# Cross-attention layer on one core: keys of two batches in one product, end columns projected ahead, block values written by DMA

## The reference, cut to what matters

```python
# 1 cross attention: 16 heads of 16 over 257 context rows, masked
k = memory @ wk.T ; v = memory @ wv.T ; q = rmsnorm(ln(x)) @ wq.T
x = x + sigmoid(h @ wg.T) * (softmax(q k^T * scale + mask) v @ wo.T)
# 2 causal self attention over 32 rows: 16 query heads, 4 key heads, rms norm and rotary on q and k,
#   ternary weights
x = x + rms_norm(attn(ln(x) @ w_qkv.T)) @ w_proj.T
# 3 feed forward of 704 with 8-bit activations and ternary weights
x = x + bitlinear(silu(bitlinear(ln(x), w1)) * bitlinear(ln(x), w3), w2)
```

## Time and profile before

| what | value |
|---|---|
| median of three runs | 576.29 us (575.0 to 815.79) |
| the profiled execution | 573.81 us |
| its span, first to last instruction | 572.0 us |
| mean granted TensorE clock | 0.993 |
| instructions | 20510 |
| DMA | 42.34 MB, mean 74 GB/s |

### The profile page before, as it was taken

One profiled execution on the slowest core, in us unless ns is written; L12 is line 12 of the kernel. 1 busy time (PEld: TensorE's weight loads), 2 busy tenths in 40 slices (PEclk: granted clock), 3 DMA queues, 4 the chain that ended last, 5 costly groups with the idle time before them and its releaser, 6 DMA issues. The chain is left out here.

```text
span 572.0 us, 20510 instructions
## 1 busy us (share of the span) xinstructions
PE 537.9 (94%) x7142; PEld 449.1 (79%) x7142; DVE 445.7 (78%) x1389; ACT 425.1 (74%) x1208; POOL 323.4 (57%) x490
## 2 busy tenths in 40 slices
PE   7898999999999999999999999999999999987785
PEld 6687788788887888888888878888888877865564
DVE  2667585888978787888979787878879776889664
ACT  5987898697878878787977787787878777773221
POOL 5241848566565748566555658475665648372610
PEclk9999999999999999999999999999999999999988
DMA  8532503214233231413142332414142404000000
GB/s 253 182 94 100 144 21 101 58 49 102 59 84 81 71 83 37 126 32 90 54 107 59 77 78 46 117 33 107 39 103 58 105 5 113 21 13 21 24 9 10
DMA packets 42805, 42.34 MB, mean 74 GB/s; under 512 B 16080, under 2 KB 33488, under 8 KB 42704
## 3 DMA queue, kind: packets, MB, share of 16 engines
q1 hardware_dynamic: 42704, 41.03, 27.3%
HBM read 38.26 MB, written 2.75 MB: 72 GB/s over the span
## 5 line engine op out<-in xcount | busy, mean ns | idle before, releaser
L874 ACT ACTIVATE pr<-sm,nb 128x257 f32<-128x257 f32 x256 | 129.2, 508 | 9.4 <-DVE nb L1110 8.0
L662 POOL TENSOR_TENSOR cTl<-cx,cTh 128x516 fp32r<-128x516 f32 x64 | 84.3, 1317 | 75.1 <-ACT cTh L771 75.0
L1110 DVE CUSTOM_DVE_ANT_0 sm<-x_ps,mbias 128x257 f32<-128x257 f32 x256 | 99.3, 419 | 21.9 <-PE x_ps L1416 20.2
L771 ACT ACTIVATE pt<-x_ps 128x512 f32<-128x512 f32 x112 | 65.3, 599 | 10.5 <-PE x_ps L1426 6.9
L1426 PE MATMUL x_ps<-tab,pr 128*128 128x128 f32 x512 | 71.4, 274 | 0.8 <-DVE o L1141 0.4
L771 ACT ACTIVATE kk<-x_ps 128x257 f32<-128x257 f32 x128 | 49.5, 389 | 22.1 <-PE x_ps L1308 22.1
L1426 PEld LDWEIGHTS x_ps<-tab,pr 128*128 128x128 f32 x512 | 57.3, 141 | 5.8 <-issue 4.4
L1308 PE MATMUL x_ps<-cTh,wkTh 128*128 128x258 f32 x256 | 59.7, 315 | 0.4 <-ACT pt L771 0.3
L670 POOL TENSOR_TENSOR sr<-sv,halfneg 128x20 f32<-128x20 f32 x16 | 56.7, 3541 | 1.3
L1308 PE MATMUL x_ps<-wvTh,cTh 128*128 128x256 f32 x256 | 56.8, 303 | 0.0
L1308 PE MATMUL x_ps<-cTl,wkTh 128*128 128x258 f32 x256 | 51.4, 282 | 0.6 <-POOL cTl L662 0.6
(11 more groups left out here) (193 smaller groups left out, 1342.7 us busy)
## 6 DMA issues: line engine op xcount, KB each, us to landing
cx<-in_ctx SPq DMA_DIRECT2D x64, 258.0 KB, 3.9
mbias<-mask_bias SPq DMA_DIRECT2D x64, 128.5 KB, 3.4
xq<-in_x SPq DMA_DIRECT2D x16, 128.0 KB, 2.9
xr<-in_x SPq DMA_DIRECT2D x16, 128.0 KB, 2.8
vx<-end_values SPq DMA_DIRECT2D x64, 32.0 KB, 2.3
vr<-self_values SPq DMA_DIRECT2D x64, 32.0 KB, 1.9
out<-yo SPq DMA_DIRECT2D x16, 128.0 KB, 2.6
fraw<-in_L_ffn_w SPq DMA_DIRECT2D x2, 704.0 KB, 5.2
```

What stands on the lines that cost most here:

```text
L662: g.tensor_tensor(cxbuf(cT[1], b)[:, :, :], cx[:, b % BT, :, :], cxbuf(cT[0], b)[:, :, :].bitcast(F32), ALU.subtract).then_inc(A_ctl, 1)
L771: return sc.activation(dst, src, ACT.Copy)
L874: sc.activation(pr[:, b % 2, gr, :], sm[:, b % 2, gr, :], ACT.Exp, bias=nb[:, n:n + 1], scale=-1.0, accum_out=st[:, 0, b, gr:gr + 1]).then ...
L1110: v.tensor_tensor_reduce(out=sm[:, b % 2, gr, :], in0=xb(f"S{b}", gr)[:, 0:LK], in1=mbias[:, b, :], scale=1.0, scalar=0.1 * NEG, op0=ALU.a ...
```

## The change

1. The context arrives with 256 columns a batch in place of 258 (the 257th and a zero). cTh and cTl have four buffers in place of two, and kk too; two neighbouring batches lie side by side, and one product of 512 columns makes the keys of both. K 1 m are batches 2 and 3 of the tile, K 2 m batches 0 and 1 of the next; K 0 m is batch 1 of tile 0 alone. So the repeated part has 24 K products of 512 columns for 48 of 258, and 4 copies of 512 columns on ScalarE for 8 of 257.
2. The keys of the 257th row are projected once for all 64 batches at the start (P_kx, 12 products of 64 columns, copied to kxs). GpSimd copies two batches' end columns from kxs into kk ahead of the query block of the first of the two. The load of the end columns and their rounding come before those of wv.
3. vr and vbd go. The four DMAs of B_shuffle write straight into blocks in wraw (free after the start), in turn into two of them, which one memset (VZ, in tile 0) has cleared. D_PV waits for the DMAs.
4. All lists, the banks and the dummy products are new: 261 dummy products for 167.

```diff
-        cx = sb("cx", [P, BT, 2, LKP])
-        cT = [sb("cTh", [P, 2, 2, LKP], F32R), sb("cTl", [P, 2, 2, LKP], F32R)]
+        cx = sb("cx", [P, BT, 2, LM])
+        cT = [sb("cTh", [P, 2, BT, LM], F32R), sb("cTl", [P, 2, BT, LM], F32R)]
-        kk = sb("kk", [P, 2, 2, LKP])
+        kk = sb("kk", [P, 2, BT, LKP])
+        kxs = sb("kxs", [P, 2, B])
...
+        def pair_of(tensor, k, p):
+            return tensor[:, k, 2 * p % BT:2 * p % BT + 2, 0:LM]
+        def vbd(n):
+            return wraw[:, n % 2 * 2:n % 2 * 2 + 2, :, :].rearrange("p a k (b c) -> p (a k) b c", b=BT)
...
-                        if due(i - 1):
-                            sp.wait_ge(B_vbd, i - 1)
+                        if due(i - 2):
+                            sp.wait_ge(B_pv, i - 2)
+                        else:
+                            sp.wait_ge(W_vz, 1)
                         for h in range(4):
-                            sp.dma_start(vr[h * S:(h + 1) * S, :, :],
+                            sp.dma_start(vbd(i)[h * S:(h + 1) * S, h, :, :],
...
+                if b % 2 == 0:
+                    if due(16 * i + 4 * b - 8):
+                        pool.wait_ge(A_ttr, 16 * i + 4 * b - 8)
+                    elif b == 0:
+                        pool.wait_ge(W_kx, 1)
+                    g.tensor_copy(kk[:, :, b:b + 2, LM:LK].rearrange("p m b c -> p m (b c)"),
+                                  kxs[:, :, BT * i + b:BT * i + b + 2]).then_inc(A_ke, 1)
+                    pool.wait_ge(A_ke, 2 * i + b // 2 + 1)
...
-            def k_out(i, b, m, ps):
+            def k_out(i, p, m, ps):
+                act.wait_ge(A_kp, 4 * i + 2 * p + m + 3)
+                if due(16 * i + 8 * p - 8):
+                    act.wait_ge(A_ttr, 16 * i + 8 * p - 8)
+                copy(pair_of(kk, m, p), ps[:, :].rearrange("p (b c) -> p b c", b=2)).then_inc(A_kh, 1)
...
+            def kproj(i, p, m, ps):
+                if m == 0:
+                    pe.wait_ge(A_ctl, 4 * i + 2 * p + 2)
+                split3(ps[:, :], lambda z, k2: wkT[z][:, k2, m * P:(m + 1) * P],
+                       lambda z, k2: pair_of(cT[z], k2, p)).then_inc(A_kp, 1)
...
-                        pe.wait_ge(A_kh, 8 * i + 2 * b + 2)
+                        pe.wait_ge(A_kh, 4 * i + (2 + 2 * b if i == 0 and b < 2 else 4 if b < 2 else 6))
...
-                        pe.wait_ge(B_vbd, i1)
+                        pe.wait_ge(L_vr, 64 * i1)
...
-                                          vbd[:, b * KV + j, :, :].rearrange("p h d -> p (h d)"), start=True, stop=True)
+                                          vbd(i1)[:, :, b, j * HD:(j + 1) * HD], start=True, stop=True)
```

```diff
+ pe first: (0, "K", 0, 0), (0, "S", 0), (0, "K", 0, 1), (0, "V", 1), (0, "GATE"), (0, "K", 1, 0), (0, "S", 1),
...
+ pe each:
+            ("S", 0), ("B_st",), ("C_xT",), ("D_QT",), ("D_kT",), ("V", 1), ("D_S",), ("S", 1), ("B_O",),
+            ("C_z", 0), ("K", 1, 0), ("B_oT",), ("K", 1, 1), ("PT", 0, 0), ("B_wo",), ("PT", 0, 1), ("V", 2),
+            ("S", 2), ("PV", 0), ("PT", 1, 0), ("PT", 1, 1), ("GATE",), ("B_xT",), ("C_z", 1), ("S", 3), ("B_qkv",),
+            ("C_z", 2), ("PV", 1), ("D_PV",), ("Q_h",), ("V", 3), ("PT", 2, 0), ("D_yT",), ("K", 2, 0),
+            ("PT", 2, 1), ("Q_q",), ("C_hT",), ("D_pj",), ("PV", 2), ("C_y",), ("K", 2, 1), ("PT", 3, 0),
+            ("PT", 3, 1), ("V", 4), ("PV", 3),
+ act each, end:
+            ("EXP", 3, 1), ("EXP", 3, 2), ("EXP", 3, 3), ("C_hT",), ("V", 3), ("Q_q",), ("K", 2, 0), ("B_keep",),
+            ("PT", 3, 0), ("K", 2, 1), ("PT", 3, 1), ("V", 4),
+ dve each, middle:
+            ("S", 1, 2), ("S", 1, 3), ("C_z", 0), ("D_s3",), ("Q_stats",), ("B_wo",), ("B_x1",), ("D_dn",),
+            ("C_h", 0), ("S", 2, 0), ("S", 2, 1), ("S", 2, 2), ("B_norm",), ("D_p3",), ("S", 2, 3), ("Q_norm",),
...
- pe last:  (17, "C_xT"), (17, "D_kT"), (17, "D_QT"), (17, "C_z", 0), (17, "D_S"),
+ pe last:  (17, "D_kT"), (17, "D_QT"), (17, "D_S"), (17, "C_xT"), (17, "C_z", 0), (17, "C_z", 1), (17, "C_z", 2),
- dve last: (16, "D_xstats"), (16, "D_xq", 0), (16, "D_xq", 1), (16, "D_xq", 2), (17, "D_scale"), (17, "D_kT"),
+ dve last: (16, "D_pj"), (17, "D_scale"), (16, "D_xstats"), (17, "D_kT"), (16, "D_xq", 0),
...
 SPARE: (17, "C_xT"): 32 -> 10, (17, "D_PV"): 28 -> 32, (18, "C_xT"): 32 -> 37, (18, "C_hT"): 28 -> 33
        and new ones before D_QT, D_kT, D_S, C_z
```

More of the change, by code:

```diff
@@ L34 @@
 LKP = LK + 1
+LM = LK - 1
 BT = P // S
@@ L58 @@
 BANK = {
[L59 to L62, removed]
[3 rows of a table removed]
-    "P_k1": (3,), "P_v": (4,), "P_vx": (5,),
+    "V1": (6,), "V2": (3,), "V3": (2,), "V4": (1,), "B_O": (0,), "B_oT": (3,), "B_wo": (5,), "B_xT": (5,),
+    "B_qkv": (5,), "D_QT": (1,), "D_kT": (3,), "D_S": (1,), "D_PV": (4,), "D_yT": (3,), "D_pj": (1,), "C_xT":
+    (6,), "C_z0": (6,), "C_z1": (2,), "C_z2": (6,), "C_hT": (4,), "C_y": (4,), "GATE": (6,), "Q_h": (5,), "Q_q":
[5 rows of a table added]
 }
@@ L104 @@
+            (2, "PT", 2, 0), (2, "K", 2, 0), (2, "D_pj"), (2, "PT", 2, 1), (2, "K", 2, 1), (2, "PT", 3, 0),
+            (2, "PV", 2), (2, "PT", 3, 1), (2, "V", 4), (2, "PV", 3),
         ],
         "each": [
-            ("S", 0), ("K", 1, 0), ("K", 1, 1), ("C_xT",), ("B_st",), ("D_kT",), ("V", 1), ("B_O",), ("D_QT",),
-            ("PT", 0, 0), ("PT", 0, 1), ("D_S",), ("S", 1), ("B_oT",), ("K", 2, 0), ("K", 2, 1), ("B_wo",),
-            ("S", 2), ("PV", 0), ("C_z", 0), ("V", 2), ("PT", 1, 0), ("K", 3, 0), ("B_xT",), ("PT", 1, 1),
@@ L127 @@
-            (15, "V", 3), (15, "PT", 2, 1), (15, "C_hT"), (15, "D_pj"), (15, "C_y"), (15, "PV", 2),
-            (15, "PT", 3, 0), (15, "PT", 3, 1), (16, "B_st"), (15, "PV", 3), (15, "GATE"), (16, "C_xT"),
-            (16, "B_O"), (16, "C_z", 0), (16, "C_z", 1), (16, "B_oT"), (16, "D_kT"), (16, "D_QT"), (16, "B_wo"),
-            (16, "D_S"), (16, "C_z", 2), (16, "B_xT"), (16, "B_qkv"), (16, "D_PV"), (16, "D_yT"), (16, "C_hT"),
-            (16, "D_pj"), (16, "C_y"), (17, "C_xT"), (17, "D_kT"), (17, "D_QT"), (17, "C_z", 0), (17, "D_S"),
@@ L132 @@
-            (17, "C_z", 1), (17, "C_z", 2), (17, "D_PV"), (17, "D_yT"), (17, "C_hT"), (17, "D_pj"), (17, "C_y"),
-            (18, "C_xT"), (18, "C_z", 0), (18, "C_z", 1), (18, "C_z", 2), (18, "C_hT"), (18, "C_y"),
+            (14, "S", 0), (14, "B_st"), (14, "D_QT"), (14, "D_kT"), (14, "V", 1), (14, "D_S"), (14, "S", 1),
+            (14, "B_O"), (14, "C_xT"), (14, "K", 1, 0), (14, "B_oT"), (14, "K", 1, 1), (14, "B_wo"),
+            (14, "PT", 0, 0), (14, "PT", 0, 1), (14, "S", 2), (14, "C_z", 0), (14, "V", 2), (14, "PV", 0),
@@ new lines @@
+            (14, "PT", 1, 0), (14, "C_z", 1), (14, "PT", 1, 1), (14, "B_xT"), (14, "D_PV"), (14, "GATE"),
[3 rows of a table added]
+            (15, "D_kT"), (14, "V", 4), (15, "B_st"), (14, "PV", 3), (15, "D_QT"), (15, "S", 1), (15, "D_S"),
[5 rows of a table added]
+            (16, "B_st"), (15, "PV", 3), (15, "D_pj"), (15, "GATE"), (16, "B_O"), (16, "D_QT"), (16, "B_oT"),
+            (16, "D_kT"), (16, "B_wo"), (16, "D_S"), (16, "C_xT"), (16, "C_z", 0), (16, "C_z", 1), (16, "B_xT"),
+            (16, "C_z", 2), (16, "B_qkv"), (16, "D_PV"), (16, "D_yT"), (16, "C_hT"), (16, "D_pj"), (16, "C_y"),
@@ L134 @@
+            (17, "D_kT"), (17, "D_QT"), (17, "D_S"), (17, "C_xT"), (17, "C_z", 0), (17, "C_z", 1), (17, "C_z", 2),
+            (17, "D_PV"), (17, "D_yT"), (17, "C_hT"), (17, "D_pj"), (17, "C_y"), (18, "C_xT"), (18, "C_z", 0),
+            (18, "C_z", 1), (18, "C_z", 2), (18, "C_hT"), (18, "C_y"),
         ],
@@ new lines @@
+            (15, "EXP", 3, 0), (15, "D_PV"), (15, "EXP", 3, 1), (15, "EXP", 3, 2), (15, "EXP", 3, 3),
+            (15, "PT", 2, 0), (15, "D_yT"), (15, "V", 3), (15, "C_hT"), (15, "PT", 3, 0), (15, "PT", 3, 1),
+            (15, "B_keep"), (15, "GATE"), (16, "B_oT"), (16, "D_QT"), (16, "C_xT"), (16, "C_z", 0), (16, "B_xT"),
+            (16, "C_z", 1), (16, "D_S"), (16, "C_z", 2), (16, "B_qkv"), (16, "D_PV"), (16, "D_yT"), (16, "C_hT"),
+            (16, "B_keep"), (17, "D_QT"), (17, "C_xT"), (17, "C_z", 0), (17, "D_S"), (17, "C_z", 1), (17, "C_z", 2),
@@ L197 @@
+            (17, "D_PV"), (17, "D_yT"), (17, "C_hT"), (18, "C_xT"), (18, "C_z", 0), (18, "C_z", 1), (18, "C_z", 2),
+            (18, "C_hT"),
         ],
@@ new lines @@
+            (16, "B_comb"), (15, "D_pj"), (16, "B_comb2"), (15, "D_xstats"), (16, "B_O"), (16, "D_scale"),
+            (16, "B_fin"), (15, "D_xq", 0), (15, "D_xq", 1), (16, "D_kT"), (15, "D_xq", 2), (16, "B_wo"),
+            (16, "B_x1"), (16, "D_S"), (16, "D_mx"), (16, "B_norm"), (16, "C_z", 0), (16, "D_s3"), (16, "C_h", 0),
+            (16, "B_xT"), (16, "C_z", 1), (16, "D_dn"), (16, "C_h", 1), (16, "D_p3"), (16, "C_z", 2), (16, "D_p4"),
+            (16, "C_h", 2), (16, "B_qkv"), (16, "C_q", 0), (16, "C_q", 1), (16, "C_q", 2), (16, "D_yT"),
```

314 lines of the change are left out of this document (149 added, 165 removed), and 107 rows, old and new, of tables (BANK, SCHEDULE).

## The result

The kernel after takes 560.35 us (median of 4 runs, 559.89 to 561.7), the kernel before 575.64 us: a ratio of 0.9755, 95% interval 0.9738 to 0.9771. (One of the four executions of the kernel before took 815.79 us; the ratio leaves it out.) It is faster, by 2.45%. The forecast was 566.0 us with a range of 556 to 575, and 0.41 for "faster". The profiled execution has a span of 559.9 us (before 572.0).

A forecast was written before the change was run, and what follows sets the result against it. TensorE's list bounds the long middle, a chain of latencies the end. Terms -5.6 - 1.2 - 1.2 + 0.7 - 1 - 2 = -10.3 gave 561.7 us of span, 566.0 us as a median; range 556 to 575.

The forecast's parts named there:

- if VectorE's waits now ended PE's: Whole kernel: one of two named signs that the forecast is wrong, beside fp32r slowing further at 512 columns.
- rival B: K products at the bf16 rate, 0.218 us each, and the new order closes TensorE's waits: 558.4 us, chance 0.20.
- the wait for xn: TensorE's 2.3 us in all before the transposes of xn; half taken as gained: -1.2 us.
- The K products: TensorE's 512-column K products at 0.230 us each: 0.36 us gained per tile, -5.6 us, from -1.9 to -10.1.
- The period: Middle tiles, by the product with wo: from 31.86 to 31.3 us; 30.9 would be B, 31.9 C.
- rival D: Slower: scores of a tile's first two batches wait for the K pair; 588 us at 1.7 us late; chance 0.07.
- rival C: Gain turns into waits on VectorE's in-order list, period stays 31.86, only start and end move: 574.0 us, chance 0.23.
- the term for entries: TensorE enters part-array steps seven times instead of eight, 0.09 us each: -1.2 us over 13 tiles.
- GpSimd's work "costed at nothing": GpSimd loses vbd, 1.97 us per tile, and gains two short copies; idle 6 us or more per tile, so 0.
- The start: End-key products +0.7 us; earlier first scores -1 us, from 0 to -3; S 0 before 17 us.
- The end: Last tiles, reordered lists: -2 us, from +1 to -4; last PV to end 54 to 57 us, was 58.
- The cover of the dummy products: End: 94 more dummies, 10 us, lie before steps that wait, so 0; each five too many cost 0.5 us.

The follow-up runs named there:

- Without the collision: Kernel after with GpSimd's cTl of batch 2 waiting for VectorE's rqk in the eleven middle tiles, so they no longer overlap: 551.19 us, ratio to before 0.9596.
- the two experiments: Kernel after without its 261 dummy products: 565.59 us; kernel after with the block values built on GpSimd again: 567.52 us.
- moving the victim: Kernel after with VectorE's product rqk moved ahead of the quantization of the feed-forward input, about 3 us earlier: 562.88 us, ratio to before 0.9758.

## Why the prediction held, and where it did not

The time fell into the range, and the change is faster, to which the forecast gave 0.41 (no clear change had 0.52). But that is in good part luck: the total came near and the sum was not right. The sign of being wrong that it named, "if VectorE's waits now ended PE's", is what happened: TensorE was to be busy over 97% of the middle with less than 2.5 us of waits, and was busy 96.0% of the ten middle tiles, with 13.6 us of waits from 105 to 455 us. 560.35 us is also nearer to rival B's 558.4 than to the 566.0 of the forecast. Of these 5.6 us the sum is to blame for 1.8 (561.7 of span for 559.9); the other 3.8 come from the step to a median, for the profiled execution of the kernel before was 2.5 us below the median of its runs and that of the kernel after is 1.35 above.

By stretches, the sum had about -5.4 us for the ten middle tiles (ten times 0.36 for K, 0.09 for entries, 0.09 for the wait for xn); measured were -0.9. For what lies behind the thirteenth product with wo it had about -3.4 (three tiles at 0.45 and 2 for the end); measured were -8.3 (142.9 to 134.6). An error of 4.5 us in the middle and errors of 4.9 us behind it and 1.7 us ahead of it, of the other sign, cancelled up to some 2 us.

- **The K products: right.** The forecast took 0.230 us apart. Measured are (296.85 - 295.36 - 0.10)/6 = 0.232 in the piece below; the median piece takes 1.48 us, which gives 0.230 and the 5.92 us a tile of the forecast:

```profile
295.36 0.71 PE L1328 MATMUL x_ps<-cTh,wkTh 128*128 128x512 f32 x2
295.91 0.63 PE L1328 MATMUL x_ps<-cTh,wkTl 128*128 128x512 f32 x2
296.38 0.63 PE L1328 MATMUL x_ps<-cTl,wkTh 128*128 128x512 f32 x2
296.85 0.38 PE L1514 MATMUL x_ps<-tab,o 128*128 128x128 f32 x2
```

  The line through the two nearer rows was a better guide than the bf16 rate of rival B. The Trainium skill (TensorE: Matmul & The Clock Gate, section Back-to-back issue gap) gives about 216 ns for a single product of 512 columns by itself and about 131 ns in a sustained stream; neither came, and the second, which the forecast did not mention, is farther off.
- **The period: wrong in the step from work to time.** It was to be 31.3 us and was 31.6 to 31.7. The wait for xn did go, all of it, but one of the same size for kap came. "A new wait" was looked for in front of S 0 only (rival D), and rival C, "the gain turns into waits", had VectorE's list as its mechanism and 0.23 as its chance. In the middle, C is what happened. Its price of 574 us was wrong because it took start and end to be worth 2.3 us, where what lies ahead of and behind the ten tiles gave 11.2. Without the collision the period is 30.74, under rival B's 30.9 without B's fast products: the sum had too small a gain in TensorE's work. It had 0.45 us a tile for K and entries, and TensorE is busy 1.0 us less. Added up from start to start over the ten tiles, steps that the sum did not price became shorter in the new order, among them the transposes of rqk (0.70 to 0.49 us a tile) and of ys in D_yT (0.36 to 0.14). Which neighbour makes them so was not tested; it includes the term for entries (-1.2).
- **GpSimd's work "costed at nothing": wrong.** I named its idle time as the cover. But idle time does not say what VectorE does while GpSimd works. The kernel before had the same meeting at another place. In its timelines one middle tile reads:

```profile
138.54 1.29 POOL L662 TENSOR_TENSOR cTl<-cx,cTh 128x516 fp32r<-128x516 f32 x1
138.64 0.42 DVE L1148 TENSOR_TENSOR o<-x_ps,o 128x256 f32<-128x256 f32 x1
139.10 1.01 DVE L1154 TENSOR_TENSOR o<-o,rden 128x256 f32<-128x256 f32 x1
```

  o times rden took 1.0 us (median of twelve 0.999, least 0.424), 0.28 us beyond the end of cTl at 139.83. In the new order this product takes 0.42 us, and rqk has the delay. Which instruction would be hit could not be read from the trace of before, but that one in each tile is hit could, and so could its price, 0.58 us there and at most the length of cTl, 1.29. The term should have had a bound on the side of a loss, some 13 x 0.58 = 7.5 us, if the hit falls on the path.
- **The start: S 0 right, the gain elsewhere.** S 0 comes at 15.67 us, "before 17" and 17.68 in the earlier trace rows. But by the first product with wo these 2.0 us are gone: it comes at 49.26 us, 48.92 in the earlier trace rows, where the sum had 0.3 gained. The 2.9 us up to the third product with wo come from the two tiles between (59.4 us for 62.6), where it had 0.9. What made them faster is open.

```profile
15.67 0.69 PE L1448 MATMUL x_ps<-kk,qbd 32*64 32x257 f32 x16
```

- **The end: its term right, the tiles ahead of it too small.** From the last PV (503.98) to the end are 55.9 us, in the forecast's 54 to 57 and 1.9 under the 57.8 of before, for which the sum had 2. The other 6.3 us lie between the thirteenth product with wo and that PV, where it had 1.35; up to the last product with wo TensorE is busy 5.0 us less (85.26 to 80.25) and the time is 7.0 shorter, so here, unlike in the middle, the saved work did become time. The cover of the dummy products held. But I costed them at 0 with the earlier trace rows, and the granted clock of 0.92 in the earlier trace rows said that there was something to gain; it is 0.99 now, and without any dummies 5.2 us are lost. The vbd products, also at 0, cost 5.7 us behind the thirteenth product in the new order. How the 8.3 us of this part divide between the clock, vbd and the reordered lists stays open: the two experiments take away from the kernel after, and the kernel before had 167 dummies and another order.

## What to carry to other kernels

An idle share of GpSimd is not free room. Before you reorder, list the VectorE instructions whose duration varies with the same form (least, median and longest side by side), look which GpSimd instruction runs beside the long ones, and price that meeting as if it fell on the critical path; to end it, order the GpSimd instruction behind the VectorE one with a wait, since moving the victim only found another here. And idle time of an engine is room only for work that stands beside the loop that ends in its wait: put a dummy in two places before you call it slack.
